# Issuing the row-maximum transfers from SyncE instead of ScalarE in a two-layer transformer kernel

## The reference

```python
mod = silu(c) @ w_adaln + b_adaln                  # shift, scale, gate for both halves
h = modulate(ln(x), sh_msa, sc_msa)
q, k, v = (h @ w_qkv + b_qkv)                      # 16 heads, 9 channels each
attn = softmax(einsum('bhqd,bhkd->bhqk', q, k) * hd ** -0.5)
x = x + g_msa * (einsum('bhqk,bhkd->bhqd', attn, v) @ w_proj + b_proj)
# layer 0: the two best of 4 experts (144 -> 576 -> 144, gelu); layer 1: one such MLP
x = x + g_mlp * mlp(modulate(ln(x), sh_mlp, sc_mlp))
```

## Time and profile before

| what | value |
|---|---|
| time, median of 3 runs | 713.84 us (711.53 to 714.16) |
| span of the profiled execution (the page gives no other time of it) | 716.4 us |
| PE busy / DVE / ACT / POOL | 530.6 / 339.5 / 266.0 / 116.3 us |
| mean granted TensorE clock | 0.786 of full |
| DMA packets of SP's queue (q1) | 50018, 41.51 MB |
| DMA packets of ACT's queue (q10) | 1088, 0.26 MB |

### The profile page before, as it was taken

How to read it: one execution, slowest core, us unless ns; L and a number is a source line. 1 busy time by engine, 2 the same in 40 slices (tenths; PEclk the granted TensorE clock), 3 DMA queues, 4 the chain that set the end, 5 groups by cost and what they waited for, 6 DMA issues and landing times.

```text
span 716.4 us, 12024 instructions
## 1 busy us (share of the span) xinstructions
PE 530.6 (74%) x4098; PEld 401.9 (56%) x4098; DVE 339.5 (47%) x1002; ACT 266.0 (37%) x549; POOL 116.3 (16%) x122
## 2 busy tenths in 40 slices
PE   6525796646837799999999995465784683879786
PEld 5313564335525456898979794343553552656575
DVE  8625234444734854261625344442571672631753
ACT  1304213432614545525261631342451451534342
POOL 8110100100100730504032151010010010000100
PEclk9955555885986657999999998565795795856999
DMA  5021362231132230000000002222132132210111
GB/s 151 16 84 80 88 149 61 85 86 75 61 90 90 74 109 2 1 17 1 0 16 1 16 6 78 86 71 84 60 99 69 70 87 72 72 37 2 34 33 50
DMA packets 51150, 42.34 MB, mean 59 GB/s; under 512 B 33345, under 2 KB 43512, under 8 KB 51102
## 3 DMA queue, kind: packets, MB, share of 16 engines
q1 hardware_dynamic: 50018, 41.51, 19.5%
q10 hardware_dynamic: 1088, 0.26, 0.2%
HBM read 33.20 MB, written 8.29 MB: 58 GB/s over the span
## 4 chain that ended last, share of the span: by engine, by line
PE 35%; issue 28%; DMA 19%; DVE 7%; SPq 6%; ACT 4%; POOL 2%; DVEq 0%; ACTq 0%; POOLq 0%
DMA KA<-qk_scratch 12%; PE bank L1388 10%; DMA QA<-mT 5%; PE bank L1189 3%; PE bank L1192 3%; PE bank L1190 3%; PE bank L1191 3%; SPq L481 3%; DMA qk_scratch<-parts 2%; PE bank L1245 2%; SPq L498 2%; POOL parts L615 2%; PE bank L1184 2%; PE bank L1234 2%; PE bank L1223 1%
## 5 line engine op out<-in xcount | busy, mean ns | idle before, releaser
L991 DVE TENSOR_REDUCE mx<-bank 128x4 f32<-128x512 f32 x128 | 86.6, 686 | 140.6 <-PE bank L1223 138.5
L743 ACT ACTIVATE pr<-bank 128x512 f32<-128x512 f32 x128 | 76.6, 598 | 179.9 <-PE bank L1234 177.6
L1223 PE MATMUL bank<-KA,QA 81*128 81x128 bf16 x512 | 64.3, 266 | 81.6 <-DMA KA<-qk_scratch 79.0
L1234 PE MATMUL bank<-QA,KA 83*128 83x128 bf16 x512 | 65.6, 267 | 50.6 <-DMA QA<-mT 50.4
L1223 PEld LDWEIGHTS bank<-KA,QA 81*128 81x128 bf16 x512 | 44.6, 120 | 101.1 <-DMA KA<-qk_scratch 55.0
L1388 PE MATMUL bank<-w_sb,hid 128*128 128x144 f32 x640 | 81.1, 286 | 0.0
L1388 PEld LDWEIGHTS bank<-w_sb,hid 128*128 128x128 f32 x640 | 79.8, 190 | 0.6
L1234 PEld LDWEIGHTS bank<-QA,KA 83*128 83x128 bf16 x512 | 46.2, 123 | 56.5 <-DMA QA<-mT 27.5
L1245 PE MATMUL bank<-pr,V 128*32 128x128 f32 x1024 | 69.2, 353 | 2.8 <-ACT pr L743 2.8
L608 POOL TENSOR_TENSOR rstd<-var_eps,minus_half 128x4 f32<-128x4 f32 x16 | 16.2, 1012 | 332.9 <-DVE var_eps L941 332.9
L826 ACT ACTIVATE hid<-bank 128x512 f32<-128x512 f32 x72 | 41.3, 602 | 50.6 <-PE bank L1192 50.6
(11 more groups left out here) (188 smaller groups left out, 959.6 us busy)
## 6 DMA issues: line engine op xcount, KB each, us to landing
QA<-qk_scratch SPq DMA_DIRECT2D x32, 324.0 KB
KA<-qk_scratch SPq DMA_DIRECT2D x96, 108.0 KB
qk_scratch<-parts SPq DMA_DIRECT2D x48, 128.0 KB, 2.3
g_mlp<-gate_scratch SPq DMA_DIRECT2D x8, 288.0 KB, 3.5
g_att<-gate_scratch SPq DMA_DIRECT2D x8, 216.0 KB, 9.2
hid<-in_L_cond_w SPq DMA_DIRECT2D x1, 1152.0 KB
w_sb<-in_L_cond_w SPq DMA_DIRECT2D x4, 288.0 KB
out<-xs SPq DMA_DIRECT2D x4, 288.0 KB, 2.4
```

The costliest lines, as they stand in the source:

```text
L743: sc.activation(pr[:, q % 2, :], bank[ST_BANK[q % 2]][:, :], ACT.Exp, scale=SCALE).then_inc(s["exp_s"], 1)
L991: v.tensor_reduce(mx[:, HQ * q:HQ * (q + 1)], bank[S_BANK[q % 2]][:, :].rearrange("p (h k) -> p h k", k=SEQ), AX.X, ALU.max).then_inc(s["m ...
L1223: last = te.matmul(bank[S_BANK[q % 2]][:, i * SEQ:(i + 1) * SEQ], QA[0:SROWS, j, h, :], KA[0:SROWS, j, h, :], start=True, stop=True)
L1234: last = te.matmul(bank[ST_BANK[q % 2]][:, i * SEQ:(i + 1) * SEQ], KA[0:MROWS, j, h, :], QA[0:MROWS, j, h, :], start=True, stop=True)
```

## The change

`m_store` moves from the ACT program to the SP program, and so does the call in the list of steps. The position in the hand-written order, MAX_STORE, is the same; the transfer is the same. It is now issued by `sp.dma_start`, in SP's order of instructions, after a wait of SP for `mt_c`.

```diff
@@ sync engine
+            def m_store(B, j):
+
+                need(sp, "mt_c", B + 1)
+                sp.dma_start(QA[SROWS:MROWS, j, :, :], mT[:, :]).then_inc(s["m_ld"], 16)
+
...
                 nxt = a if start else a + 1
+                if what == "MAX_STORE":
+                    m_store(G * a + i, i % G)
                 if what == "QK_PARTS":
                     store_parts(nxt, i)
@@ scalar engine
-            def m_store(B, j):
-
-                need(act, "mt_c", B + 1)
-                act.dma_start(QA[SROWS:MROWS, j, :, :], mT[:, :]).then_inc(s["m_ld"], 16)
-
...
-                if what == "MAX_STORE":
-                    m_store(G * a + i, i % G)
```

## The result

The changed kernel takes 727.76 us (median of 4 runs, 724.48 to 730.44) against 712.68 us (median of 4, 704.90 to 714.16). The ratio is 1.025, with a 95% interval of 1.020 to 1.030: slower by 18 us, 14 to 21. By the medians it is +15.1. The forecast was 730, within 720 to 741.

A forecast was written before the change was run, and what follows sets the result against it. The prediction took the kernel to be bound by its DMAs in attention, with stores sharing the loads' engines. Layer starts 8 and 6.5 plus loop bodies 2 gave +16.5, say +16, on the median 713.84: 730 us, range 720 to 741.

The forecast's parts named there:

- Store 0 lands behind load 3: Start of layer 0: store 0 lands with the gates at about 77.5, S(0) moves from 64.22 to 77.6.
- The start of layer 0, +8: Layer 0 up to load 8: load 4 +6.4, shift of the DMA chain +7.5, load 8 is 8 us late.
- load 7 keep its distance to load 6: Layer 0's first group: load 7 and the next writes keep their distances behind load 6, so the chain shifts +7.5.
- The start of layer 1, +6.5: Layer 1 up to load 20: S(16) +14.1, load 20 at 492.9 against 486.08, taken as +6.5, bounds 5 and 14.
- The loop bodies, +2.0: Loop groups: late S(9) and S(10) hidden; 0.65 us a group for the second store's issue, three sets, +2.0.
- The slack ahead of store 11: Loop body: store 11 goes at 221.8 behind load 13, S(11) at its old time with 2 us to spare.
- The last groups, 0 and -0.4: Layers' last groups, without scratch writes: layer 0 costs 0, at most +5; layer 1 perhaps -0.4.
- The sum: Whole kernel: 8 + 6.5 + 2 = +16.5, say +16, giving 730 from the median of the runs.
- order in a queue does not matter: Rival, chance 0.09: a store on SP's queue takes 7.34 us as on ACT's; 719 in all.
- The loop groups do not hide it: Rival, chance 0.08: the spare 2 us ahead of store 11 are used up, 3 us lost per group; 745.
- Faster: Rival, chance 0.03: on SP stores no longer wait behind ACT's other copies, 0.4 us in ten to twelve places; -4, 710.

The follow-up runs named there:

- The first experiment: Only stores 0 and 16, at the layers' starts, issued by SP, the other 30 by ACT; 728.04 us against 711.99 for the kernel before, ratio 1.023.
- third: Only the third store of each group but the layers' last groups issued by SP; 715.66 us against 711.99 for the kernel before, ratio 1.0025.
- fourth experiment: Only the second store of each group but the layers' last groups issued by SP; 711.81 us against 711.99 for the kernel before, ratio 1.002.
- the second experiment: All stores but 0 and 16 issued by SP, those two by ACT; 716.56 us against 711.99 for the kernel before, ratio 1.006.
- the one with shorter loads: All stores on SP, QA's load as three DMAs and KA's as nine; 639.76 us, against 609.48 with the same loads and stores on ACT.

## Why the prediction was right

*Store 0 lands behind load 3.* Right: 77.02 for S(0), forecast 77.6; the landing of the gates in the kernel before had been the right row to read. The first experiment and the one with the store ahead of the third load show it from both sides.

*The start of layer 0, +8.* Load 4 +5.3 (6.4), S(2) at 112.8 (111), the gate write at 125.92 (127.5), S(3) at 130.47 (131.5), load 6 +6.7 (7.5), load 8 +9.1 (8). Load 4 is less late than forecast partly because store 1 was issued (87.67 to 88.35) before the last part was ready (88.76), so that its 0.7 us cost nothing. The agreement at load 8 is partly luck. The prediction let load 7 keep its distance to load 6, and that step was wrong: load 7 needs the slot of block 3, whose scores were last read at 140.14, and was issued at 140.72, 14.4 us late. It was 126.32 before, right behind the last scores of block 3 too. The scratch writes, which wait for load 7, came 23.1 us behind load 6 instead of 20.1. These 3 us stand against 0.8 that load 6 came ahead of its forecast, and 1.2 at the writes, which with store 5 among them took 0.6 less than before where 0.6 more was forecast.

*The start of layer 1, +6.5.* 11.1 - 5.3 = 5.8 from load 16 to load 20.

*The loop bodies, +2.0.* +1.6 for loads 8 to 12, +0.1 for 20 to 24, +0.5 for 24 to 28: 2.2 in all. The number can't be told from chance: the kernel with untouched loop bodies shows differences of that size too (+1.0, +0.8 and -0.4). That late S(9) and S(10) are nearly hidden was right, and the times of the single experiments on the second and the third store confirm it. The slack ahead of store 11 held: S(11) begins at 233.22 without waiting for its store, 9.4 us later than before, about as much as load 8 (9.1).

*The last groups, 0 and -0.4.* In layer 1 the shift goes from 11.8 us at load 28 to 11.0 at the end. In layer 0 it goes from 10.3 us at load 15 to 5.3 at load 16: 5 us came back, which the prediction had not foreseen.

*The sum.* 9.1 + 5.8 + 2.2 = 17.1, forecast 16.5; the timed runs say 15 by the medians and 18 by the ratio. With the 5 us that came back the profiles differ by 11 us only. So the match of the sum with the timed runs holds for three of its parts, and rests on leaving out the fourth. Where the 5 us went can be read: PE works nearly all the time there, and the granted clock rose earlier. The kernel before, then the changed one:

```profile
272.00:276.00 4.00, 4.00 (x19) 2.59 (x18) 0.62 (x2) 0.79 (x2) 0.00 (x0) 0.50 0.00 0
276.00:280.00 4.00, 4.00 (x20) 3.01 (x19) 0.91 (x4) 3.05 (x6) 0.00 (x0) 0.95 0.01 2
```

```profile
273.00:277.00 4.00, 3.78 (x50) 2.37 (x50) 3.06 (x11) 2.36 (x6) 0.00 (x0) 0.90 0.34 76
```

Before, the clock was at 0.50 (1.2 GHz) until about 276 us though PE had not paused from 260 on; after, it was at full speed (2.4 GHz) from about 274, where the program stood 9 us further back.

Whether the change had a part in that stays open. From load 15 to load 16 it is 205.0 us in the kernel before, and 205.8, 205.0 and 202.2 in the first, third and fourth experiment, which leave the stores of the last group as they were. It is 200.1 in the changed kernel, 200.9 and 200.6 in the second experiment and the one with the store ahead of the third load, and 200.7 with stores right behind the copy, and these four all issue the stores of the last group otherwise. That speaks against the luck of one execution. On the other side, every timed run is about 1.8 us longer than its span; by that, as an estimate, the profiled execution before took 718 us, 5 above its median, and the changed one was 1.4 above its own. So the gap between 11 and 15 us lies in a long execution of the kernel before, and a usual one may not have the late rise. The prediction took 2.6 us for this distance, because it set a span against a time; its 730 was the median and 16, and does not depend on it.

*The rivals.* That order in a queue does not matter is out by S(0): it came 12.8 us later, and only 5.0 of these were the later issue. "The loop groups do not hide it" was wrong for this kernel and right for the one with shorter loads: there a group took 5.5 to 6 us more, with the clock as a possible part. "Faster" had a gain of about 3 us, but on ACT.

What I had not seen is the other half of program order: SP's later loads wait for mT behind the store. The prediction named it for the scratch writes only. In this kernel no run shows a cost of it.

## What to carry to other kernels

Look twice before a small transfer that an engine waits for is issued by the engine that issues bulk loads: here it landed behind what was issued ahead of it, and what stood behind it in the program waited for its data. Most such stores cost nearly nothing, because PE had a load to wait for anyway; two of 32, at the starts of the layers, cost about the whole 2.5%. If a store must be there, try its place in the order: ahead of the third load instead of behind the fourth, S(0) started at 62.28 instead of 77.02. And before moving a small DMA away from a slow one, look why the big one is slow: a source repeated three times inside one DMA held it on three engines, and splitting both loads was worth 102 us.

## What the hardware showed unexpectedly

- Splitting a DMA made its issue cheaper for each piece, and dearer in all: QA's 81 rows with a repeated source took 0.72 us to issue, three DMAs of 27 rows 1.0 us together; KA's three with a repeated source took 2.1 us, nine of 9 rows 3.2 us.
- Issues took longer where four loads were issued close together: the three KA issues of load 3 took 7.0 us instead of 2.1, and store 0 behind them 2.14 us instead of 0.7.
- Runs of one kernel spread by 1 to 3% here, and the granted clock's rise at the end of layer 0 came 30 us behind load 15 in some profiles and 43 us behind it in others (the kernel before: 43), which moves a profile by 4 to 5 us. A term of 0.65 us was seen in the trace and not in 12 timed runs.
